# Bidirectional Mamba stage of a language-model layer: one addition moved from VectorE to ScalarE, VectorE's work merged and reordered, the fusion product moved, and the dt projection in two row groups

## The reference, cut to what matters

```python
def _mamba(x, Win, convw, convb, Wx, Wdt, bdt, Alog, Dp, Wout):
    u, z = jnp.split(jnp.einsum('bld,ed->ble', x, Win), 2, axis=-1)
    up = jnp.pad(u, ((0, 0), (D_CONV - 1, 0), (0, 0)))
    uc = convb
    for k in range(D_CONV):                      # 4 taps
        uc = uc + up[:, k:k + Ln, :] * convw[:, k]
    uc = _silu(uc)
    x_dbl = jnp.einsum('bld,ed->ble', uc, Wx)    # 16 dt rows, 32 B rows, 32 C rows
    dt = softplus(jnp.einsum('blr,dr->bld', x_dbl[..., :DT_RANK], Wdt) + bdt)
    ...
        h = exp(dt_t[..., None] * A) * h + (dt_t * u_t)[..., None] * B_t[:, None, :]
        y = jnp.einsum('bdn,bn->bd', h, C_t)
    ...
    return jnp.einsum('bld,ed->ble', (ys + uc * Dp) * _silu(z), Wout)
fo = _layernorm(_mamba(x, forward weights))
bo = _layernorm(_mamba(x reversed, backward weights) reversed)
out = concatenate([fo, bo]) @ Wfuse.T + bfuse
```

## Time and profile before

| | |
|---|---|
| runs | 5065.68, 5070.26, 5071.86 us |
| median | 5070.26 us |
| profiled execution, time | 5086.73 us |
| profiled execution, span | 5084.8 us |
| mean granted TensorE clock | 0.898 of full |
| span: TensorE, VectorE, ScalarE, GpSimd busy | 87%, 81%, 50%, 47% |
| Mamba stage within the span | up to about 2712 us |
| one sequence (two slots) in the middle of the stage | 81.9 us |

### The profile page before, as it was taken

One profiled execution on the slowest core, in us unless ns is written; L12 is line 12 of the kernel. 1 busy time (PEld: TensorE's weight loads), 2 busy tenths in 40 slices (PEclk: granted clock), 3 DMA queues, 4 the chain that ended last, 5 costly groups with the idle time before them and its releaser, 6 DMA issues. The chain is left out here.

```text
span 5084.8 us, 78746 instructions
## 1 busy us (share of the span) xinstructions
PE 4435.8 (87%) x21916; PEld 3270.1 (64%) x21917; DVE 4132.0 (81%) x8064; ACT 2554.3 (50%) x4137; POOL 2400.0 (47%) x2014
## 2 busy tenths in 40 slices
PE   5999999999999999999897888888888649998998
PEld 3555555555555555555555666666666549898988
DVE  6999999999999999999994666666666547777876
ACT  4666656666666656666663333333434224444343
POOL 2434444343434444344533555555555545555555
PEclk8888888888888888888887999999999879999999
DMA  1011101010111111011111111211112135544554
GB/s 53 29 27 35 29 27 32 24 32 24 33 25 35 30 28 32 24 32 24 33 24 46 55 66 67 71 64 64 63 68 68 62 101 87 87 84 83 89 85 77
DMA packets 182184, 257.01 MB, mean 51 GB/s; under 512 B 23121, under 2 KB 126674, under 8 KB 182002
## 3 DMA queue, kind: packets, MB, share of 16 engines
q1 hardware_dynamic: 121074, 157.34, 10.8%
q0 software_dynamic: 60928, 98.09, 9.9%
HBM read 138.76 MB, written 116.59 MB: 50 GB/s over the span
## 5 line engine op out<-in xcount | busy, mean ns | idle before, releaser
L521 PE MATMUL pj<-xt,win 128*128 128x512 f32 x3144 | 874.4, 430 | 228.6 <-DVE uc L703 225.4
L521 PEld LDWEIGHTS pj<-xt,win 128*128 128x128 f32 x3144 | 617.1, 202 | 452.4 <-DVE uc L703 265.0
L291 POOL TENSOR_TENSOR wk<-v,uc 128x512 f32<-128x512 f32 x260 | 392.1, 1508 | 1060.7 <-DVE v L753 1060.7
L1931 POOL DMA_INDIRECT out<-e_y,e_to x272 | 442.5, 1627 | 429.5 <-DVE e_y L2078 361.4
L703 DVE SCALAR_TENSOR_TENSOR uc<-pj,convw,uc 128x511 f32<-128x511 f32 (+2 forms) x780 | 517.3, 734 | 65.3 <-issue 59.7
L1981 PE MATMUL e_p<-e_w,e_a 128*128 128x256 f32 x3264 | 422.3, 287 | 42.7 <-DVE e_a L2071 42.7
L568 PE MATMUL po<-yz,wout 128*128 128x512 f32 x1024 | 449.9, 592 | 0.0
L1969 PE MATMUL e_p<-e_xt,e_w 128*128 128x256 f32 x3264 | 411.7, 283 | 39.5 <-DVE e_xt L2059 39.2
L1981 PEld LDWEIGHTS e_p<-e_w,e_a 128*128 128x128 f32 x3264 | 402.7, 195 | 44.2 <-DVE e_a L2071 44.2
L1969 PEld LDWEIGHTS e_p<-e_xt,e_w 128*128 128x128 f32 x3264 | 392.2, 189 | 48.3 <-issue 47.6
L1145 POOL DMA_INDIRECT expert_in<-a_xs,a_idx x256 | 249.6, 975 | 301.1 <-DVE a_flag L1549 208.1
(11 more groups left out here) (251 smaller groups left out, 9588.6 us busy)
## 6 DMA issues: line engine op xcount, KB each, us to landing
e_x<-expert_in SPq DMA_DIRECT2D x137, 260.0 KB
bb<-bc SPq DMA_DIRECT2D x65, 512.0 KB, 4.8
a_h<-h_rows SPq DMA_DIRECT2D x136, 128.0 KB
h_rows<-h1o SPq DMA_DIRECT2D x32, 512.0 KB, 5.4
a_hb<-h_rows SPq DMA_DIRECT2D x128, 128.0 KB
out<-a_bs SPq DMA_DIRECT2D x128, 128.0 KB
bc<-xd SPq DMA_DIRECT2D x65, 128.0 KB, 2.2
e_w1s<-in_moe_w POOLq DMA_DIRECT2D x10, 512.0 KB
```

Source lines behind the costliest of these rows:

```text
L291: pool.tensor_tensor(wk[:, m, :], v[:, m, :], uc[d][:, m, :], ALU.mult).then_inc(S["dtu_ok"], 1)
L521: i = mm(pj[m][:], win[d][wp][:, k, c:c + P], xt[xp][:, k, :], start=(k == 0 and n == 0), stop=(k == KD - 1 and n == 2))
L1931: pool.indirect_dma_start(out=out, out_offset=bass.IndirectOffsetOnAxis(ap=to[n][:, j:j + 1].bitcast(U32), axis=0), in_=y[n][:, j, :], in_ ...
```

## The change

The edits, all in the Mamba stage:

1. VectorE's addition w = 1 + y (L742) is gone. A new function `softplus_sum` does it on ScalarE as an Identity with bias 1, between the exponential and the logarithm. Exponential, sum and logarithm run as two 128x1024 operations each instead of four 128x512 ones, and the logarithm reads w.
2. `outputs` is one 128x2048 operation, and stands ahead of `more_states`. The last operation of the softplus is one 128x2048 operation (`softplus_end`), the last of the slot, and `dead_mask` stands just ahead of it. `hc_ok` and `dt_ok` count once a pass.
3. `project_copies` moves on ScalarE from behind `decays` and the table load to between the two halves of `last_tap_and_bias`.
4. TensorE: `dt_proj` moves ahead of `row_squares`; `out_proj` moves between the two parts of the `u` half; `fusion` runs in the same slot as the `out_proj` of its pass, as the last of the slot.
5. `dt_proj` reads the dt rows from two places: tiles 0 and 2 from rows 64 to 79, tiles 1 and 3 from rows 96 to 111. For that `Wx` has the dt columns twice with 16 columns of zeros between, `Wdt` is loaded twice, and `x_dbl` and its copy make 112 rows instead of 80.
6. GpSimd waits in `d = 1` for the end of `dead_test` of pass `t + 1` ahead of `keep_residual` and `gather`.

```diff
+DT_ROWS = (2 * NS, 3 * NS)
+NXR = DT_ROWS[1] + RK
...
-                sp.dma_start(wdt[d][2 * NS:NX, :], k["Wdt"]).then_inc(S["ld_w"], 16)
+                for at in DT_ROWS:
+                    sp.dma_start(wdt[d][at:at + RK, :], k["Wdt"]).then_inc(S["ld_w"], 16)
...
-                    pool.wait_ge(S["dt_ok"], NP * t + m // 2 + 1)
+                    pool.wait_ge(S["dt_ok"], t + 1)
...
                     if d == 1:
+                        pool.wait_ge(S["gt_ok"], 2 * t + 4)
                         keep_residual(s + 1)
                         gather(s + 2)
...
-                act.activation(xd[d][0:NX, :], px[0:NX, :], ACT.Copy).then_inc(S["xd_ok"], 1)
+                act.activation(xd[d][0:NXR, :], px[0:NXR, :], ACT.Copy).then_inc(S["xd_ok"], 1)
...
             def softplus_exp(t):
-                for m in range(MD):
-                    act.wait_ge(S["vc_ok"], MD * t + m + 1)
+                for h in range(NP):
+                    mm = slice(2 * h, 2 * h + 2)
+                    act.wait_ge(S["vc_ok"], MD * t + 2 * h + 2)
                     if not (isinstance(t, int) and t == 0):
-                        act.wait_ge(S["h_ok"], MD * (t - 1) + m + 1)
-                    act.activation(y[:, m, :], lg[:, m, :], ACT.Exp, scale=-1.0).then_inc(S["y_ok"], 1)
+                        act.wait_ge(S["h_ok"], MD * (t - 1) + 2 * h + 2)
+                    act.activation(y[:, mm, :], lg[:, mm, :], ACT.Exp, scale=-1.0).then_inc(S["y_ok"], 1)
+
+            def softplus_sum(t):
+                for h in range(NP):
+                    mm = slice(2 * h, 2 * h + 2)
+                    act.wait_ge(S["y_ok"], NP * t + h + 1)
+                    if not (isinstance(t, int) and t == 0):
+                        act.wait_ge(S["tp_ok"], MD * (t - 1) + 2 * h + 2)
+                    act.activation(wk[:, mm, :], y[:, mm, :], ACT.Identity, bias=1.0).then_inc(S["w_ok"], 1)
 
             def softplus_log(t):
-                for m in range(MD):
-                    act.wait_ge(S["y_ok"], MD * t + m + 1)
-                    act.activation(lg[:, m, :], y[:, m, :], ACT.Ln, bias=1.0).then_inc(S["l_ok"], 1)
+                for h in range(NP):
+                    mm = slice(2 * h, 2 * h + 2)
+                    act.wait_ge(S["w_ok"], NP * t + h + 1)
+                    act.activation(lg[:, mm, :], wk[:, mm, :], ACT.Ln).then_inc(S["l_ok"], 1)
...
-            def back(t, d):
+            def back(t, d, copies):
 
-                last_tap_and_bias(t + 1, 1 - d)
+                last_tap_and_bias(t + 1, 1 - d, range(2))
+                if copies:
+                    project_copies(t - 1)
+                last_tap_and_bias(t + 1, 1 - d, range(2, MD))
                 decays(t, d)
...
-                    mm(pj[m][:], wdt[d][2 * NS:NX, m * P:(m + 1) * P], xd_rows(d), start=True, stop=True
+                    rows = slice(DT_ROWS[m % 2], DT_ROWS[m % 2] + RK)
+                    mm(pj[m][:], wdt[d][rows, m * P:(m + 1) * P], xd[d][rows, :], start=True, stop=True
...
                 in_proj(t, d, 1, range(2, MD))
+                dt_proj(t, d)
                 if back > 1:
                     row_squares(t - 2)
-                dt_proj(t, d)
                 if turn:
                     turn_x(s_next)
-                if back > 1:
-                    fusion(t - 2, d)
                 state_sum(t)
                 dead_sums(t, d)
                 pe.wait_ge(S["xl_ok"], KD * (s_next + 1))
                 in_proj(t + 1, 1 - d, 0, range(2))
                 dead_count(t)
+                if back > 0:
+                    out_proj(t - 1, 1 - d)
                 in_proj(t + 1, 1 - d, 0, range(2, MD))
                 if back > 0:
-                    out_proj(t - 1, 1 - d)
+                    fusion(t - 1, 1 - d)
...
-                    ts(wk[:, mm, :], y[:, mm, :], 1.0, None, ALU.add).then_inc(S["w_ok"], 1)
...
-                for h, mm in pairs():
-                    dve.wait_ge(S["d0_ok"], NP * t + h + 1)
-                    stt(v[:, mm, :], v[:, mm, :], 0.0, wk[:, mm, :], ALU.max, ALU.add).then_inc(S["dt_ok"], 1)
+
+            def softplus_end(t):
+
+                dve.wait_ge(S["d0_ok"], NP * (t + 1))
+                stt(v[:], v[:], 0.0, wk[:], ALU.max, ALU.add).then_inc(S["dt_ok"], 1)
...
-                for h, mm in pairs():
-                    dve.wait_ge(S["h_ok"], MD * t + 2 * h + 2)
-                    tt(tp[:, mm, :], tp[:, mm, :], over_pair(bb[d][:, 1, :]), ALU.mult).then_inc(S["hc_ok"], 1)
+                dve.wait_ge(S["h_ok"], MD * (t + 1))
+                tt(tp[:], tp[:], bb[d][:, 1, :].unsqueeze(1).to_broadcast([P, MD, SEQ]), ALU.mult
+                   ).then_inc(S["hc_ok"], 1)
...
                     bc_product(t + 1, 1 - d)
+                    outputs(t, d)
                     more_states(t, d)
-                    outputs(t, d)
...
+                    softplus(t + 1)
                     dead_mask(t + 1, 1 - d)
-                    softplus(t + 1)
+                    softplus_end(t + 1)
...
-        out[f"Wx{d}"] = np.concatenate([wx[RK:], wx[:RK]]).T
+        out[f"Wx{d}"] = np.concatenate([wx[RK:], wx[:RK], np.zeros((NS - RK, DI), wx.dtype), wx[:RK]]).T
```

More of the change, by code:

```diff
@@ L69, in mamba_stage @@
         win = [[sb(f"win{d}{h}", [P, KD, 2 * DI], F32R) for h in range(2)] for d in range(DIRS)]
-        wx = [sb(f"wx{d}", [P, MD, NX]) for d in range(DIRS)]
+        wx = [sb(f"wx{d}", [P, MD, NXR]) for d in range(DIRS)]
         wdt = [sb(f"wdt{d}", [P, DI]) for d in range(DIRS)]
@@ L182, in broadcast @@
                 if not (isinstance(t, int) and t < 2):
-                    wait_apart(sp, S["hc_ok"], NP * (t - 1))
+                    wait_apart(sp, S["hc_ok"], t - 1)
                 wait_apart(sp, S["xd_ok"], t + 1)
@@ L323, in _ @@
         def _(act):
-            act.wait_ge(S["ld_w"], 16 * (12 * DIRS + 1))
+            act.wait_ge(S["ld_w"], 16 * (13 * DIRS + 1))
             for d in range(DIRS):
@@ L346, in xt_copy, with last_tap_and_bias @@
                     act.activation(xt[0][:, k, :], pj[k][:], ACT.Copy).then_inc(S["xt_ok"], 1)
-            def last_tap_and_bias(t, d):
+            def last_tap_and_bias(t, d, tiles):
                 tap = TAPS - 1
-                for m in range(MD):
+                for m in tiles:
                     act.wait_ge(S["u_ps"], MD * t + m + 1)
@@ L392, in softplus_exp @@
             def softplus_exp(t):
-                for m in range(MD):
-                    act.wait_ge(S["vc_ok"], MD * t + m + 1)
+                for h in range(NP):
+                    mm = slice(2 * h, 2 * h + 2)
+                    act.wait_ge(S["vc_ok"], MD * t + 2 * h + 2)
                     if not (isinstance(t, int) and t == 0):
-                        act.wait_ge(S["h_ok"], MD * (t - 1) + m + 1)
-                    act.activation(y[:, m, :], lg[:, m, :], ACT.Exp, scale=-1.0).then_inc(S["y_ok"], 1)
+                        act.wait_ge(S["h_ok"], MD * (t - 1) + 2 * h + 2)
[7 more added lines that the diff above has]
+                    act.activation(wk[:, mm, :], y[:, mm, :], ACT.Identity, bias=1.0).then_inc(S["w_ok"], 1)
             def softplus_log(t):
-                for m in range(MD):
-                    act.wait_ge(S["y_ok"], MD * t + m + 1)
-                    act.activation(lg[:, m, :], y[:, m, :], ACT.Ln, bias=1.0).then_inc(S["l_ok"], 1)
+                for h in range(NP):
+                    mm = slice(2 * h, 2 * h + 2)
+                    act.wait_ge(S["w_ok"], NP * t + h + 1)
+                    act.activation(lg[:, mm, :], wk[:, mm, :], ACT.Ln).then_inc(S["l_ok"], 1)
             def decays(t, d):
                 for m in range(MD):
-                    act.wait_ge(S["dt_ok"], NP * t + m // 2 + 1)
+                    act.wait_ge(S["dt_ok"], t + 1)
                     act.activation(y[:, m, :], v[:, m, :], ACT.Exp, scale=amat[d][:, m, 0:1]).then_inc(S["da_ok"], 1)
@@ L455, in _ @@
             act.preload_act_table_set("silu_and_others")
-            last_tap_and_bias(0, 0)
+            last_tap_and_bias(0, 0, range(MD))
             front(0, 0)
@@ L459, in _ @@
             softplus_exp(0)
+            softplus_sum(0)
             softplus_log(0)
-            back(0, 0)
+            back(0, 0, False)
             def slots(s, first):
@@ L474, in slots @@
                     softplus_exp(t + 1)
+                    softplus_sum(t + 1)
                     softplus_log(t + 1)
-                    back(t + 1, 1 - d)
-                    project_copies(t)
+                    back(t + 1, 1 - d, True)
             slots(0, True)
@@ L488, in _ @@
             pe.wait_ge(S["c_tab"], 5)
-            pe.wait_ge(S["ld_w"], 16 * (12 * DIRS + 1))
+            pe.wait_ge(S["ld_w"], 16 * (13 * DIRS + 1))
             pe.wait_ge(S["prep_w"], 1)
@@ L529, in x_dbl @@
                     pe.wait_ge(S["uc_ok"], MD * t + m + 1)
-                    i = mm(px[0:NX, :], wx[d][:, m, :], uc[d][:, m, :], start=(m == 0), stop=(m == MD - 1))
```

(5 more changed lines are left out.)

7 lines of the change are left out of this document (3 added, 4 removed).

## The result

The changed kernel takes 4937.89 us (median of 4 runs, 4923.93 to 4955.66) against 5070.38 for the kernel before on the same chip: a ratio of 0.9742, 95% interval 0.9714 to 0.9769, so 132 us less. The forecast was 4987 in a range of 4915 to 5072: the side was right, and the gain was 49 us larger than forecast. The narrower range that the forecast gave for its own case, 4955 to 5020, does not hold the measured time. The profiled execution of the changed kernel took 4923.93 us (span 4922.3).

What follows compares the result with a forecast made beforehand. VectorE was taken to set the pace; its terms summed to 4.8 us a sequence, but a new wait for ScalarE in `d = 1` left 2.6 for each of 32 sequences, 83 us: 4987 us, range 4915 to 5072.

Steps and rivals of the forecast that it cites:

- L742 gone: VectorE's addition in the softplus: removing it saves 1.20 us a slot, 2.4 a sequence.
- The scan freed: VectorE's last scan in `d = 1` no longer stands still for GpSimd's addition: 2.1 us, net 1.6 a sequence.
- `dead_count`: VectorE's wait for it ahead of `dead_mask` ends once that moves behind two softplus pairs: 0.6 us a sequence.
- Merges: Two VectorE pairs become one operation each in both slots: 0.07 us for each merge, 0.2 net a sequence.
- The loop's jump: VectorE's 2.14 us idle time ahead of a sequence's first convolution operation stays: gain 0, bounds 0 and 1.1.
- The branch of `more_states`: VectorE's branch over the further states showed no idle time in any slot, so moving it gains nothing.
- ScalarE's chain: Softplus on ScalarE: first logarithm ready 4.8 us after the first exponential starts, instead of 3.3; bounds 4.2 and 5.4.
- TensorE's tail: Queue behind `finish`: `out_proj`, second `u` part, `fusion`, 13.4 us; `z` starts 6.3 us into `d = 1`, VectorE waits about 2.2.
- Everything stays hidden: Rival, chance 0.18: TensorE-ScalarE chain ends 2 us earlier, VectorE remains the only bound; 4.5 to 4.8 us a sequence, about 4922.
- The tail at the low clock: Rival, chance 0.17: after TensorE idles ahead of `out_proj`, 22 passes run slow, 4.4 us later; 5115 us in all.
- The branch laid bare: Rival, chance 0.07: `more_states` branch behind `outputs` late by 1.2 to 1.8 us in `d = 0`; about 5035 us.
- Nothing to measure: Rival, chance 0.05: low clock in part of TensorE's tail leaves 5070 us.

Runs made afterwards that it cites:

- nowait: The changed kernel with GpSimd's wait for the dead test taken out again; 4971.8 us, ratio 0.9799 to the kernel before.
- pwait: The kernel before with only GpSimd's new wait for the dead test ahead of the residual's addition; 5185.0 us, ratio 1.0228.
- rowvar: The changed kernel with ScalarE's `row_var` behind the first two tiles of `v_copy` instead of ahead of them; 4907.4 us, ratio 0.9678 to the kernel before.
- oldpe: The changed kernel with TensorE's order of before and `project_copies` behind `decays` again; 4895.2 us, ratio 0.9665 to the kernel before.
- short: The kernel before with VectorE's never-executed block of further states written for one tile instead of four; 5035.4 us, ratio 0.9937.
- ahead: The changed kernel with 24 small memsets, executed once, ahead of VectorE's loop; 4959.6 us, ratio 0.9789 to the kernel before.
- sum: The kernel before with only w = 1 + y moved to ScalarE and its softplus steps in halves of 128x1024; 4924.2 us, ratio 0.9716.

## Why the prediction was right, and what was mis-sized

- **L742 gone: right.** In `d = 0` VectorE comes to the first pair 32.39 us into the slot (1041.33 less 1008.94); the forecast was 32.4.
- **The scan freed: right in mechanism.** All of the 2.1 us came back; the 0.5 us that I took off for the pair beside GpSimd fell into the wait, as the text allowed. nowait prices the wait at 34 us; alone, ahead of an untouched softplus, it costs 115 (pwait). I had costed the queue behind it at nothing because `scan_inputs` would have time. That was luck in part: in the changed kernel the copy falls into VectorE's wait, and where that wait is gone (rowvar, oldpe) the scan inputs come late and cost 0.5 us in `d = 0`.
- **`dead_count`: right.** The wait is gone. **Merges: 0.07 us for each of three** (L770 takes 2.20 from start to start, the pair was 2.27; `outputs` in `d = 0` 2.32 instead of 2.39) and nothing for `outputs` in `d = 1` (2.33, before 2.28), some 0.16 a sequence of 0.2 forecast: right and small.
- **The loop's jump: this term is the one that failed.** Forecast 0, bounds 0 to 1.1; measured 2.0 to 2.1 us a sequence, 62 to 65 us over 31 jumps. short and ahead show that in the changed kernel it is no matter of the cover: the fetch itself is gone, by where the loop lies. With the fetch back (ahead) the idle time is 0.9 and not 2.0, so even then the term would have been near its upper bound of 1.1 and not 0. The Trainium skill, "Runtime: NRT & Kernel Launch", the part on instruction fetch, says that a taken branch waits for a fetch when its target is outside the window of two pages. The prediction read that as saying that a jump over so long a body must fetch. Here the same body fetches (170 packets) or does not (20), which the sentence allows, as it goes by where the target lies; what failed is the step from the long body to a target that is always outside.
- **The branch of `more_states`: right.** No idle time behind `outputs`.
- **ScalarE's chain: right.** First exponential to first pair: 1075.04 to 1080.03, 4.99 us (forecast 4.8). **`dt_proj`: 1.99** (2.15).
- **TensorE's tail: right in mechanism, 1.4 us short** in the slot shown. Timeline of TensorE:

```profile
1041.54 8.83 PE L587 MATMUL po<-yz,wout 128*128 128x512 f32 x16 [1.67 <-DVE h1o L857]
1049.81 3.36 PE L539 MATMUL pj<-xt,win 128*128 128x512 f32 x12
1053.01 3.62 PE L608 MATMUL po<-wfus,fo 128*128 128x256 f32 x16
1056.28 3.14 PE L539 MATMUL pj<-xt,win 128*128 128x512 f32 x12
...
1077.62 7.13 PE L587 MATMUL po<-yz,wout 128*128 128x512 f32 x16 [0.45 <-DVE h0c L857]
```

`out_proj` takes 8.27 from start to start instead of 6.9, behind 1.67 us of idle time; behind 0.45 the same 16 passes take 7.13, about as in the earlier trace rows. The clock was at its lower level in the middle of it (a stretch of two us, columns as in the earlier trace rows):

```profile
1043.00:1045.00 2.00, 2.00 (x3) 0.68 (x2) 2.00 (x3) 0.00 (x0) 0.00 (x0) 0.50 0.00 0
```

At 0.20 more a slow pass that is some seven to nine passes. `z` begins 7.9 us into the slot instead of 6.3, and `v_copy` 22.1 instead of 20.6:

```profile
1069.48 0.26 ACT L345 ACTIVATE r<-pss,eps 128x4 f32<-128x4 f32 x1 [1.90 <-PE pss L598]
1070.47 0.69 ACT L389 ACTIVATE v<-pj,bdt 128x512 f32<-128x512 f32 x1 [0.72 <-issue]
```

That is the chain as forecast, and 1.5 us of it carry through to L761 (31.65 into the slot instead of 30.2). Without the 2.1 us of the jump the forecast slot is 37.4. In 21 of 30 slots of the stage `out_proj` takes 7.13 and the slot 37.0 to 38.1, 37.5 in the mean; in the other 9 `out_proj` takes 8.8 and the slot 38.7 to 38.9. So the low clock in this place costs 0.4 us on average, as was allowed.

**The sum.** Forecast 2.6 a sequence; 2.1 of the jump more makes 4.7; measured 4.50. Over 31 sequences that is 139 us; the medians differ by 132. (The profiled executions differ by 163: the one of before stood 16.5 us above its median, and the later stages of the two, which the change does not touch, differ by some 20.)

**The rivals.** *Everything stays hidden* gave nearly the measured time (4922), but not by its mechanism: the wait for the logarithm is there, and rowvar and oldpe, which remove it, go 30 and 43 us lower. *The tail at the low clock* happened in 9 slots of 30, to about half of its threshold of 15 slow passes, and did not decide. It expected 4 us of idle time ahead of `out_proj` and the bet against it rested on the length of that time, but the length alone does not tell: in all nine slots it was 1.67 or 1.68 us, and one of the others has the same 1.67 with fast passes, as the earlier trace rows have 2.02. Timeline of TensorE in the changed kernel, 390 us earlier:

```profile
652.39 7.13 PE L587 MATMUL po<-yz,wout 128*128 128x512 f32 x16 [1.67 <-DVE h1o L857]
```

What decides is open.

*The branch laid bare* did not occur. *Nothing to measure* fell. The forecast's own range, 4955 to 5020, does not follow from the bounds that it names: 1.3 us of `dt_proj` upward and 0.6 of the activations either way, over 32 sequences, give 4968 to 5048.

## What to carry to other kernels

Price a stall at a loop's jump as a matter of its own: look at the instruction queue's packets in both profiles, since removing ten instructions (four in the loop, six ahead of it) ended it and adding 24 brought it back. A small operation of a second engine should be put where the first engine waits, not only away from the operation that it disturbed: the same wait on GpSimd cost 115 us in one order and gained 34 in the other. When work is moved from the pacing engine, run that edit alone before reordering others to serve it. Here it brought as much as the whole change (some 62 us of it by the loop's new place), and the reordering of TensorE and ScalarE took 43 us back.

## What the runs showed of the hardware

- One loop of VectorE either loads instructions at each of its jumps (170 packets; 3.6 us from the branch to the next record in before, 2.9 in ahead) or at none (about 20 packets, 0.32 us), with the same executed work in the loop (before and short; changed and ahead). A kernel measured beside another can differ by this alone.
- One addition of GpSimd of 128x1024 lengthens a pair of VectorE operations with two inputs in SBUF by 1.0 to 2.2 us (1.0 in rowvar, 1.5 in sum, 2.2 in nowait); in the scan of the earlier trace rows and in these it is VectorE's operation that began later that stood. That is not the whole rule: in pwait a 128x4 copy of GpSimd stood for 8.03 us through a row of VectorE operations, seven of which began after it, and in rowvar and oldpe it took 0.90 beside the same kind of operations.
- Eight passes of 16 rows took 1.99 us from two row groups and 4.30 to 4.93 from one (part of these at the low clock; 3.4 by the 0.43 us of a pass at full clock).
